# GpSimd's bias-and-residual sum in the two feed-forwards waits for VectorE's normalised tiles of the next group

## What is computed

```python
def _layer(x, wqkv, qs, ksc, wo, lg, lb, w1, b1, w2, b2):
    ...
    x = x + o @ wo
    h = shift_token(x)
    mu = h.mean(-1, keepdims=True)
    var = h.var(-1, keepdims=True)
    h = (h - mu) / jnp.sqrt(var + 1e-05) * lg + lb
    h = h @ w1 + b1
    a, g = jnp.split(h, 2, axis=-1)
    h = a * jax.nn.gelu(g, approximate=False)
    x = x + h @ w2 + b2
    return x
```

## Time and profile before

| what | value |
|---|---|
| median of 3 runs | 2032.74 us (2032.38 to 2032.87) |
| the profiled execution | 2034.3 us, its span 2032.5 us |
| PE busy | 1713.9 us (84%), x12344 |
| DVE busy | 1543.8 us (76%), x4148 |
| ACT busy | 1360.1 us (67%), x4708 |
| POOL busy | 883.5 us (43%), x824 |
| mean granted TensorE clock | 0.921 of full speed |
| first normalised tile of f0 to the last sum into F | 1145.85 to 1228.91 us |
| first normalised tile of f1 to the last sum into F | 1606.81 to 1697.15 us |

### The profile page before, as it was taken

The page is one execution under the profiler, slowest core; times in us unless marked ns, Lnnn a source line. Parts: engine busy times, 40 slices in busy tenths (PEclk is TensorE's granted clock), DMA queues, the critical chain, the costliest instruction groups (busy, mean ns, idle before and its releaser), DMA issues. The chain is left out here.

```text
span 2032.5 us, 39197 instructions
## 1 busy us (share of the span) xinstructions
PE 1713.9 (84%) x12344; PEld 1131.0 (56%) x12410; DVE 1543.8 (76%) x4148; ACT 1360.1 (67%) x4708; POOL 883.5 (43%) x824
## 2 busy tenths in 40 slices
PE   4999999999999955899999696899999686754991
PEld 2555555555555532677777353577777443552660
DVE  2898898988898974899999365899999484663445
ACT  2888888888888863788888223688888344322555
POOL 3555565555555543333333123333333143285554
PEclk9999999999999986999999897999999897755996
DMA  6991000000000000000000110000000110012324
GB/s 203 187 179 22 2 1 2 1 2 2 2 2 2 2 1 6 11 12 17 17 12 17 29 24 6 12 12 17 17 12 17 26 27 2 7 44 70 82 65 133
DMA packets 102525, 65.90 MB, mean 32 GB/s; under 512 B 27698, under 2 KB 93874, under 8 KB 102322
## 3 DMA queue, kind: packets, MB, share of 16 engines
q1 hardware_dynamic: 97970, 54.40, 13.3%
q0 software_dynamic: 4352, 8.99, 1.3%
HBM read 19.50 MB, written 30.24 MB: 24 GB/s over the span
## 5 line engine op out<-in xcount | busy, mean ns | idle before, releaser
L411 ACT ACTIVATE a_E<-a_psS,a_nm 128x128 f32<-128x128 f32 (+1 forms) x1028 | 418.8, 428 | 31.4 <-DVE a_nm L245 28.9
L216 POOL TENSOR_SCALAR a_aT<-a_dT 128x384 f32<-128x384 f32 x256 | 309.5, 1209 | 298.9 <-PE a_psO L529 187.4
L245 DVE TENSOR_REDUCE a_nm<-a_psS 128x2 f32<-128x256 f32 (+1 forms) x514 | 260.2, 547 | 43.6 <-PE a_psS L496 42.9
L492 PE MATMUL a_psS<-a_kT,a_qm 32*128 32x128 f32 (+1 forms) x2064 | 240.6, 351 | 5.6 <-issue 3.6
L270 DVE SCALAR_TENSOR_TENSOR a_d<-a_E,a_cf 128x128 f32<-128x128 f32 (+1 forms) x512 | 219.3, 468 | 27.9 <-DVE a_cf L259 1.4
L411 ACT ACTIVATION_READ_ACCUMULATOR a_E<-a_psS,a_nm 128x1 f32 x1028 | 219.8, 214 | 0.0
L788 POOL TENSOR_TENSOR b0rn<-b0ss,minus_half 128x16 f32<-128x16 f32 x36 | 107.1, 2975 | 223.9 <-DVE b0ss L824 223.9
L788 POOL TENSOR_TENSOR b1rn<-b1ss,minus_half 128x16 f32<-128x16 f32 x36 | 107.1, 2976 | 223.2 <-DVE b1ss L824 223.2
L420 ACT ACTIVATE a_dT<-a_psT 128x384 f32<-128x384 f32 x256 | 126.7, 495 | 74.3 <-PE a_psT L505 71.3
L492 PEld LDWEIGHTS a_psS<-a_kT,a_qm 32*128 32x128 f32 x2064 | 136.6, 186 | 55.7 <-issue 35.4
L505 PE MATMUL a_psT<-ident,a_d 128*128 128x128 f32 x768 | 132.4, 281 | 6.2 <-DVE a_d L270 0.4
(11 more groups left out here) (353 smaller groups left out, 4408.5 us busy)
## 6 DMA issues: line engine op xcount, KB each, us to landing
mx_rows<-mx_blank SPq DMA_DIRECT2D x9, 2080.0 KB, 32.0
mx_xin<-mx_rows SPq DMA_DIRECT2D x72, 65.0 KB, 2.0
b0v<-b0v SPq DMA_DIRECT2D x34, 128.0 KB, 2.3
b1v<-b1v SPq DMA_DIRECT2D x34, 128.0 KB, 2.4
F<-mx_results SPq DMA_DIRECT2D x8, 256.0 KB, 4.9
mx_second<-mx_results SPq DMA_DIRECT2D x8, 256.0 KB, 5.4
out_dram<-X SPq DMA_DIRECT2D x8, 256.0 KB, 2.3
f0z<-F SPq DMA_DIRECT2D x9, 128.0 KB
```

The costliest lines, as they stand in the source:

```text
L216: pool.tensor_scalar(aT[:, s, :], dT[:, s, :], 0.0, None, ALU.max).then_inc(positived.sem, 1)
L245: ins = dve.tensor_reduce(nm[:, s, t, :], psS[:, s, :, (0, P)[t]:(P, 384)[t]], axis=AX.X, op=ALU.max, negate=True)
L411: ins = act.activation(E[:, s, m, c0:c1], psS[:, s, m, c0:c1], ACT.Exp, bias=nm[:, s, t, m:m + 1], accum_out=Z[:, p, h, t, m:m + 1])
L492: pe.matmul(psS[:, s, m, c0:c1], qm[rows, p, a, r, t * P:(t + 1) * P], kT[rows, p, a, 0:c1 - c0], start=(t == 0), stop=False)
```

## The change

In each batch GpSimd now waits, after `rstd` and ahead of fb, until VectorE has written the last of the four normalised tiles of the next group. A semaphore `waited`, which nobody waits for, is raised by a small instruction behind the two waits. No operation on data is added, removed or resized, and no instruction changes its place.

```diff
-        zeroed = sem("zeroed")
+        zeroed, waited = sem("zeroed"), sem("waited")
...
             for pair in range(PAIRS):
                 for half in range(2):
                     rstd(pair, half, 1)
+
+                    pool.wait_ge(xn_ready.sem, xn_ready.at(pair, half, 1))
                     pool.wait_ge(added.sem, added.at(pair, half, 0))
+                    pool.sem_inc(waited, 1)
                     pool.tensor_tensor(fb[:, :, :], f_of(pair, half), b2[:, :].unsqueeze(1).broadcast_to([P, NT, D]),
                                        ALU.add).then_inc(fb_ready.sem, 1)
                     normalise_groups(2 * pair + half)
```

## The result

The changed kernel takes 2014.17 us in the median of 6 runs (2012.29 to 2017.54). The kernel before took 2033.49 us in the median of its 6 (2032.38 to 2037.93). The ratio is 0.9901, 95% interval 0.989 to 0.9912: 1.0% faster, about 20 us. Two later sets of runs gave the same ratio, 0.9901. One execution of the kernel before in a later set took 3385.55 us, for no known reason, and is left out of the ratios. The prediction had the sign and the mechanism of the stalls right; its 15.6 us were too few by about 4. The median, 2014.17, is at the very end of its range of 2014.1 to 2022.1; on the 2032.74 us that the forecast started from, the ratio gives 0.9901 x 2032.74 = 2012.6 us, just outside it. The profiled execution took 2013.99 us, its span fell from 2032.5 to 2012.2 us.

A forecast was written before the change was run, and what follows sets the result against it. VectorE's tiles, stalled by GpSimd's sums, were taken to delay psY and bound both feed-forwards. Gains of 4.97 in f0 and 10.67 in f1, 15.64 us, took the 2032.74 us median to 2017.1, range 2014.1 to 2022.1.

The forecast's parts named there:

- The stall, and that it moves psY: Both feed-forwards: VectorE's tiles stand still until GpSimd's sums end, 0.92 us beside one, 1.87 beside two, delaying u and psY.
- A + 2.78: TensorE's psY start without the stall, 2.78 us after A, the start of the last psA pair; batch 0 measured it.
- 4.97 and 10.67 us: Gains from the stalls: f0 seven batches at 0.71; f1 one at 0.71 and six at 1.66.
- the slow spell: f1's batch 6: psY took 4.57 us instead of 2.94 at a low granted clock, 1.63 us in the profiled execution.
- What is queued behind the wait costs nothing: GpSimd's fb, X and f1's powers still come in time; at worst 5.0 us would be given back.
- the first 0.17 to spare: f1: the X sum ends at A + 3.78, 0.17 us before VectorE's small L634 at A + 3.95.
- u and the statistics are not held: VectorE's u1, u2 and layernorm statistics, now beside fb and X, are not slowed: cost nothing, u staying at 0.75 us.
- Rival 2: The stall moves to u, delaying u2 and psY in both feed-forwards: 11 us slower, 2043.7; chance 0.03.
- SP's shifts: SP's queue, one shift per 8.66 us at its limit, keeps pace with the new 8.99 us period.
- The clock: f1: 1.63 us of slow clock goes from the profiled execution; the runs' median, 1.56 lower, was taken as without it.
- The sum: Whole kernel: 15.64 us from the stalls and 1.63 from the clock, 2034.3 to 2017.0 profiled; 2017.1 forecast for the median.
- quicker hand-overs: Term of the range's low end: hand-overs 0.1 us quicker in 14 batches, 1.4 us.

The follow-up runs named there:

- half_fb: Kernel before without the wait, GpSimd's bias sum covering only two of the four tiles of a group: ratio 0.9965.
- x_waits: Kernel before with only f1's X sum waiting for the tiles, fb left where it was in both feed-forwards: ratio 0.9966.
- wait_gated: Changed kernel with GpSimd's wait put later, behind the third gated product u instead of behind the tiles: ratio 0.9937 to the kernel before.
- last_u_late_2: Changed kernel, psY's first two products started ahead of the wait for the third u, second set: ratio 0.9864 to the kernel before.
- last_two: Kernel before with the wait only in batches 6 and 7 of both feed-forwards: ratio 0.9971.
- fill: Kernel before, stalls left in, with one more 128x512 product on TensorE while it would wait for the tiles: ratio 0.9989.
- before_again: Kernel before, unchanged, profiled a second time: f1's slow psY came again, one batch earlier, and b1's first part took 61.30 us.
- first_six: Kernel before with the wait only in batches 0 to 5 of both feed-forwards: ratio 0.9941.

## Why the prediction was right and wrong

- **The stall, and that it moves psY:** right. Tiles 1.10, psY at A + 2.78, period 9.00; half_fb and x_waits show the cause.
- **4.97 and 10.67 us:** right, measured 4.93 and, with the slow spell, 12.31 for 12.30.
- **What is queued behind the wait costs nothing:** right, but nearer than said: fb started 0.21 after the tiles and not 0.1, and 0.06 us of the first 0.17 to spare were left. wait_gated shows what comes beyond it, 0.84 us a batch.
- **u and the statistics are not held:** right, u took at most 752 ns with fb beside it (the median went from 740 to 751). Rival 2 fell.
- **SP's shifts:** right, the queue kept pace with 9.00 and with 8.55. The 8.66 us that the prediction took for the queue's limit was one pair of issues; in last_u_late_2 some follow each other after 8.34 us.
- **The clock, wrong:** the step "the median of the runs is 1.56 lower, as if they had not had the slow spell". The spell came in every profile of a kernel with whole stalls in f1, so the timed runs must be taken to have it too, and 1.63 had to come off their median as well: 2032.74 - 15.64 - 1.63 = 2015.5. I took a difference between one execution and a median for a sign of a mechanism, where runs of one kernel differ by 5 to 6 us.
- **The sum, wrong by a missing term:** the stages behind the feed-forwards were booked at nothing. They gave 1.72 in b1, 0.41 at the barrier ahead of the state space and 0.5 behind it in the first pair of profiles, and 1.0 to 2.0 us in b1 over all pairs. With both, 2032.7 - 15.6 - 1.6 - 2.6 = 2012.9, against 2012.6 by the ratio. The range's low end held the slow spell's 1.6 us and 1.4 for quicker hand-overs, which did not come (fb started later than reckoned, not earlier), but nothing for these stages.

**What stays open.** The 1 to 2 us in b1 belong to the change of f0 and go with the moment at which the granted clock falls, in all fifteen profiles of the table. What sets that moment is not shown: filling TensorE's pause in f0 did not move it as expected, the columns fit f0's length, and no run tells length from the speed of the last batches. The 0.41 us at the barrier go with the added semaphore and have no known cause. The 0.5 us behind the state space is open; the stretch is at 37.4 to 37.6 in the six profiles where the clock holds 4.6 us or more after f1, and at 37.8 to 38.6 in the nine others.

## What to carry to other kernels

Where the same instruction on VectorE has two lengths, look at what GpSimd does at the longer one's start: if it ends with GpSimd's instruction, a wait on GpSimd that costs its own chain nothing can take the stall off VectorE's. Before adding it, count what stands behind that wait on GpSimd's list; here the room was 0.06 us and then 0.25. And where a change shortens a stage, book the clock of the stage behind it as a term with bounds, since the end may lie elsewhere between two changes of the clock, and judge a slow spell by a second profile, not by the distance from one execution to a median.

## What the runs showed of the hardware

- A VectorE tensor_scalar from SBUF to SBUF that starts while a GpSimd sum runs lasts until that sum ends, at both sizes seen: up to 1.28 us for 128x128 beside one sum in f0, 1.20 for 128x4 (0.33 and 0.17 alone). scalar_tensor_tensor with one input from PSUM (at most 752 ns) and the batch-norm statistics (0.86 us for four) were not held.
- GpSimd's sum of 128x256 took 0.73 us, of 128x512 1.27.
- TensorE's granted clock fell to 0.50 between 2.3 and 3.6 us after the end of f0's last psY in the profiles with 9.16 or 9.70 us in f0's last batches, and 4.5 to 5.0 us after it in those with 9.00 or 8.55. Behind f1 this did not hold: 2.3 us in last_two with quick last batches, 4.2 in fill with stalled ones.
- Executions of one kernel on one chip lay up to 6 us apart (2030.64 to 2036.71 in one set of the kernel before), for a cause that is not shown. One stretch that no change here touches, from the first scattered rows of the last stage to its first results, took 107.2 to 107.7 us in the four profiles of the set with before_again and 101.9 to 103.4 in the other sets but that of first_six and last_two (105.5 and 107.4), so it differs more between sets than within them.
